# Layer 1's value product in a two-layer transformer kernel: the first key tile in three rounded products

## The chip, the core and the metric

The kernel runs on one NeuronCore of one Trainium2 chip. The metric is the device time of one execution in microseconds; the median of 3 runs of the kernel before is 726.27 us (725.91 to 726.91). The engines work side by side and meet by semaphores: TensorE (PE) multiplies and transposes, VectorE (DVE) and ScalarE (ACT) work element by element, GpSimd (POOL) prepares weights, SyncE (SP) starts the loads. Results of TensorE arrive in PSUM, which has eight banks here used for one purpose each.

## The reference, cut to what matters

Four sequences of 256 tokens with 256 features pass through two pre-norm layers of attention and feed-forward. The change is in layer 1's attention: 16 heads of 128, causal.

```python
k = jnp.einsum('ihd,bpd->biph', W_K, x)
q = jnp.einsum('ihd,bpd->biph', W_Q, x)
v = jnp.einsum('ihd,bpd->biph', W_V, x)
scores = jnp.einsum('biph,biqh->biqp', k, q)
mask = jnp.tril(jnp.ones((pos, pos), dtype=x.dtype))
masked = scores * mask - jnp.float32(10000000000.0) * (1.0 - mask)
attn = jax.nn.softmax(masked / jnp.sqrt(jnp.float32(d_head)), axis=-1)
z = jnp.einsum('biqp,biph->biqh', attn, v)
z_flat = jnp.transpose(z, (0, 2, 1, 3)).reshape(b, pos, -1)
out = jnp.einsum('df,bqf->bqd', W_O, z_flat)
```

## The kernel before

The attention of a layer is 64 units: 8 head pairs, and in each pair 4 sequences times 2 heads. A unit is one sequence and one head, 256 queries against 256 keys. Since the mask is causal, the first tile of 128 keys meets all 256 queries and the second only the last 128, so probabilities are 384 columns a unit. All engines run the same sequence of slots, numbered -5 to 70. Slots -5 to 10 are written out, slots 11 to 58 are three rounds of a loop of 16 slots, and the rest is written out again. In slot c each engine works on several units at different ages: TensorE does the scores of unit c, the query/key projection and the value projection of step c + 5, the output projection of unit c - 6 (from slot 6 on), the transposes of the probabilities of unit c - 2, and the value product of unit c - 3, in that order. What orders the engines among each other are counting semaphores: `need` waits until a step of a unit is done. Each engine goes through its own list strictly in order, so a wait holds up all that stands behind it.

Weights and normalised tokens are held as two fp32r tensors each, a main part (hi, the value rounded to fp32r) and a remainder (lo, the difference, also rounded). A product of two such values is three products: hi by hi, hi by lo, lo by hi (`PASSES`). Scores and value products are plain fp32. A value projection writes bank 4 (`TQ_BANK`), and ScalarE copies it to `v` (L454); TensorE may write the next one once that copy is done (`vev`). The turned probabilities go to bank 5 (`PT_BANK`) and ScalarE copies them to `probs_t` (L412). The value product (L330 for the first key tile, L332 for the second) adds into bank 6, from where ScalarE takes the main part of the encoded values (L425) and VectorE the remainder (L500). VectorE's slot is: normalise the probabilities of unit c - 1 (L480, L483), add the output to the residual (L491), `enc_lo` (L500), maxima of the scores of unit c (L519).

At slots -4 to -2 of layer 1 the end of layer 0's feed-forward still runs on VectorE and TensorE: the sparse selection (work, L921 to L929) and the last down-projection (L723). L382 is layer 1's query/key projection, L396 its value projection, L304 the output projection, L316 the transposes, L282 and L283 the scores.

Of the kernel before, what the change touches and what calls it, by code (L numbers as in the profile page):

```python
# [29 lines left out]
P = 128  # L30
D = 256
# [20 lines left out]
SECOND_OUTPUT_FROM, SECOND_OUTPUT_TQ = UNITS - 10, UNITS - 6  # L52
HI_HI, HI_LO, LO_HI = (0, 0), (0, 1), (1, 0)
# [17 lines left out]
def need_pairs(eng, sem, it, c, per_pair):  # L71

    if it is not None:
        eng.wait_ge(sem, it * (2 * per_pair) + c)
    elif c > 0:
        eng.wait_ge(sem, c)

def build(nc, x_in, wa, wax, wb, wdown0, w2t, consts, scales, out):
    with ExitStack() as ctx:  # L80
# [3 lines left out]
        def sem(name):  # L84
# [28 lines left out]
        rot_a = sb("rot_a", [P, 2, 384])  # L113
        rot_b = sb("rot_b", [P, 2, 384])
        cos_t = sb("cos_t", [P, 2, 3, DH])
        sin_t = sb("sin_t", [P, 2, 3, DH])

# [29 lines left out]
        w2_a = sb("w2_a", [P, 8, D])  # L147
        w2_b = work[:, 0:8 * D].rearrange("p (a d) -> p a d", d=D)
# [10 lines left out]
                 "a0hi", "a0", "ahi", "a", "bhi", "b")  # L159
# [126 lines left out]
        def pe_output(pe, L, it, c):  # L286
# [3 lines left out]
            if live(it, m):  # L290
# [6 lines left out]
                elif m == SECOND_OUTPUT_TQ:  # L297
                    pe.wait_ge(s["tqev" if L == 0 else "vev"], UNITS)
                elif m > SECOND_OUTPUT_FROM:
                    pe.wait_ge(s["opadd"], m - 1)  # L300
                else:
                    need(pe, s["opadd"], it, m)
# [5 lines left out]
        def pe_turn_probs(pe, L, it, c):  # L308
# [3 lines left out]
            if live(it, m):  # L312
                need(pe, s["pnorm"], it, 2 * m + 2, 2)
                need(pe, s["ptev"], it, m)
                for j in range(3):
# [3 lines left out]
        def pe_values(pe, L, it, c):  # L319
# [3 lines left out]
            if live(it, m):  # L323
# [6 lines left out]
                pe.matmul(bank[O_BANK][:, 0:256], v[:, m // 8 % 2, 2 * b, vc:vc + DH], probs_t[:, m % 2, 0:256],  # L330
                          start=True, stop=False, skip_group_check=True)
# [16 lines left out]
        def pe_slot(pe, L, it, c):  # L348
# [38 lines left out]
            if L == 1:  # L387

                m = c + 5
                if live(it, m):  # L390
# [3 lines left out]
                    need(pe, s["vev"], it, m)  # L394
                    for i, (g, (l, r)) in enumerate([(g, p) for g in range(NC) for p in PASSES]):
# [10 lines left out]
        def act_turned(act, L, it, m):  # L406

            s = at[L]
            if live(it, m):
                need(act, s["pt"], it, m + 1)  # L410
                need(act, s["pv"], it, m - 1)
                nc.scalar.copy(probs_t[:, m % 2, :], bank[PT_BANK][:, 0:384]).then_inc(s["ptev"], 1)  # L412

        def act_slot(act, L, it, c):
# [12 lines left out]
            if live(it, m):  # L427
# [8 lines left out]
                else:  # L436
# [14 lines left out]
                    elif it is None and m == 8:  # L451

                        act.wait_ge(ff[0]["down"], 12)
                    nc.scalar.copy(v[:, m // 8 % 2, t, :], bank[TQ_BANK][:, 0:D]).then_inc(s["vev"], 1)  # L454
# [47 lines left out]

        def dve_scores_wait(dve, L, it, c):
# [19 lines left out]
        def dve_slot(dve, L, it, c):  # L523
            s = at[L]
            if c < TAIL_SLOT:
                dve_normalise(dve, L, it, c)
                dve_residual(dve, L, it, c)
                dve_scores_wait(dve, L, it, c)
# [12 lines left out]
            if live(it, m):  # L541
                t = m % 8
                if L == 0:
# [932 lines left out]
```

## Time and profile before

| | |
|---|---|
| median of 3 runs | 726.27 us |
| the profiled execution, its own time | 726.39 us |
| its span | 724.6 us |
| TensorE busy | 702.7 us, 97% |
| VectorE busy | 495.1 us, 68% |
| ScalarE busy | 407.7 us, 56% |
| GpSimd busy | 353.3 us, 49% |
| chain that ended last | TensorE 93% |

Busy times of TensorE come from records that overlap, since a product begins before the one ahead has drained; spacing of starts, or the chain of waits, tells what a product costs. "PEld" is the loading of weights, which runs beside the products. An fp32 product is recorded as two instructions of each kind. A line number names the line of the kernel that issued the instruction. "idle before" is how long the engine stood ahead of an instruction, and the releaser is what it waited for.

### The profile page before, as it was taken

The numbers are of one execution on the slowest core, as the hardware profiler recorded it, in microseconds if no ns is written. First come the engines' busy times: TensorE is split into PE (matmuls) and PEld (weight loads), VectorE is DVE, ScalarE is ACT, GpSimd is POOL, SyncE is SP. The second block draws the span as 40 slices with busy tenths as digits, with TensorE's granted clock in tenths as the row PEclk, the third lists the DMA queues.
The fourth block names the chain that finished last, engine by engine and source line by source line (L and its number), as shares of the span: only waits on it lengthen the run. The fifth ranks groups of instructions, "written<-read, shape, count | busy, mean of one in ns | idle before, by whom it ended". The sixth has DMA issues, their size and how long they took to land.

```text
span 724.6 us, 14870 instructions
## 1 busy us (share of the span) xinstructions
PE 702.7 (97%) x4296; PEld 627.5 (87%) x4296; DVE 495.1 (68%) x1698; ACT 407.7 (56%) x1214; POOL 353.3 (49%) x503
## 2 busy tenths in 40 slices
PE   4799999999999998999999999999999999999998
PEld 3589999999999997788889999999999999987887
DVE  6998888888888889869755554444444444587443
ACT  4576666667676674523246555555555555664221
POOL 3898888878888853202069842323232323018000
PEclk9999999999999999999999999999999999999999
DMA  6010210101020010100021010101010200000000
GB/s 232 2 44 2 103 45 1 43 0 43 0 101 29 29 67 7 45 1 0 16 88 59 1 59 1 59 7 52 14 44 26 75 0 0 0 1 1 1 30 29
DMA packets 9002, 24.64 MB, mean 34 GB/s; under 512 B 896, under 2 KB 3072, under 8 KB 8832
## 3 DMA queue, kind: packets, MB, share of 16 engines
q1 hardware_dynamic: 8240, 22.55, 8.9%
q10 hardware_dynamic: 720, 1.57, 0.6%
q8 instruction: 21, 0.34, 0.2%
q14 instruction: 21, 0.17, 0.1%
HBM read 23.07 MB, written 1.05 MB: 33 GB/s over the span
## 4 chain that ended last, share of the span: by engine, by line
PE 93%; DVE 3%; POOL 1%; issue 1%; DMA 1%; ACT 0%; ACTq 0%; DVEq 0%; POOLq 0%
PE bank L382 12%; PE bank L664 12%; PE bank L304 12%; PE bank L376 11%; PE bank L330 7%; PE bank L283 7%; PE bank L396 6%; PE bank L316 6%; PE bank L282 4%; PE bank L332 4%; PE bank L703 3%; PE bank L345 3%; PE bank L707 2%; PE bank L723 1%; PE bank L243 1%
## 5 line engine op out<-in xcount | busy, mean ns | idle before, releaser
L471 ACT ACTIVATE probs<-scores,negmax 128x128 f32<-128x128 f32 (+1 forms) x256 | 115.5, 452 | 40.8 <-DVE negmax L519 40.1
L500 DVE TENSOR_TENSOR enc_lo<-bank,enc_hi 128x256 fp32r<-128x256 f32 x128 | 54.2, 424 | 116.7 <-PE bank L283 113.2
L412 ACT COPY probs_t<-bank 128x384 f32<-128x384 f32 x128 | 61.3, 479 | 122.8 <-PE bank L316 122.8
L565 POOL TENSOR_TENSOR a_hi<-raw_a,zero 128x384 fp32r<-128x384 f32 (+1 forms) x60 | 43.7, 728 | 86.8 <-PE bank L396 86.8
L483 DVE TENSOR_SCALAR probs<-probs,rinv 128x128 f32<-128x128 f32 (+1 forms) x256 | 80.8, 357 | 4.5
L330 PE MATMUL bank<-probs_t,v 128*128 128x256 f32 x256 | 76.6, 381 | 0.1
L283 PE MATMUL bank<-qk 128*128 128x256 f32 x256 | 76.5, 380 | 0.0
L229 POOL TENSOR_TENSOR ln_r<-ln_ve,neg_half 128x1 f32<-128x1 f32 x24 | 15.5, 644 | 123.8 <-DVE ln_ve L207 123.8
L578 POOL TENSOR_TENSOR rms_r<-meansq,neg_half 128x3 f32<-128x3 f32 x64 | 58.3, 911 | 34.5 <-DVE meansq L555 34.3
L304 PE MATMUL bank<-b_hi,enc_hi 128*128 128x256 f32 x256 | 74.3, 290 | 0.2 <-DVE x L491 0.2
L304 PE MATMUL bank<-b_hi,enc_lo 128*128 128x256 f32 x256 | 72.3, 282 | 0.0
L304 PE MATMUL bank<-b_lo,enc_hi 128*128 128x256 f32 x256 | 72.3, 282 | 0.0
L376 PE MATMUL bank<-a_hi,xT_hi 128*128 128x512 f32 x128 | 62.3, 486 | 4.9 <-DVE xT_lo L256 4.0
L580 POOL TENSOR_TENSOR rot_a<-rot_a,rot_b 128x384 f32<-128x384 f32 x64 | 66.4, 1038 | 0.0
L316 PE MATMUL bank<-cst,probs 128*128 128x128 f32 x384 | 63.0, 272 | 0.0
L425 ACT CAST enc_hi<-bank 128x256 fp32r<-128x256 f32 x128 | 47.6, 372 | 25.5 <-PE bank L332 25.4
L382 PE MATMUL bank<-xT_hi,a_hi 128*128 128x512 f32 x128 | 61.5, 481 | 0.3 <-DVE xT_lo L256 0.3
L567 POOL TENSOR_TENSOR a_lo<-raw_a,a_hi 128x384 fp32r<-128x384 f32 (+1 forms) x60 | 54.8, 914 | 4.7
L332 PEld LDWEIGHTS bank<-probs_t,v 128*128 128x128 f32 x256 | 48.6, 190 | 6.6
L491 DVE TENSOR_TENSOR x<-bank,x 128x256 f32<-128x256 f32 x128 | 53.1, 415 | 0.0
L304 PEld LDWEIGHTS bank<-b_hi,enc_hi 128*128 128x128 f32 x256 | 48.4, 189 | 4.4 <-issue 0.3
L304 PEld LDWEIGHTS bank<-b_lo,enc_hi 128*128 128x128 f32 x256 | 48.3, 189 | 4.4
(130 smaller groups left out, 2056.5 us busy)
## 6 DMA issues: line engine op xcount, KB each, us to landing
raw_a<-in_wa SPq DMA_DIRECT2D x10, 768.0 KB, 4.4
raw_a<-in_wa SPq DMA_DIRECT2D x9, 512.0 KB, 4.2
raw_b<-in_wb SPq DMA_DIRECT2D x16, 256.0 KB, 2.6
x<-in_x SPq DMA_DIRECT2D x4, 256.0 KB, 5.8
hid_last<-in_wax SPq DMA_DIRECT2D x2, 512.0 KB, 4.8
w_a<-in_w2t SPq DMA_DIRECT2D x1, 1024.0 KB, 4.8
raw_b<-in_wdown SPq DMA_DIRECT2D x2, 512.0 KB, 3.3
raw_a<-in_wa ACTq DMA_DIRECT2D x1, 512.0 KB, 5.1
```

What stands on the lines that cost most here:

```text
L283: pe.matmul(ps[:, 128:384], qk[:, q, t0 + 128:t0 + 256], qk[:, k, t0:t0 + 256], start=True, stop=True).then_inc(s["scores"], 1)
L304: mm = pe.matmul(output_bank(m)[:, 0:D], enc[l][:, h, t * P:(t + 1) * P], b_w[slot][r][:, h * D:(h + 1) * D], start=i == 0, stop=i == 5)
L316: mm = pe.transpose(bank[PT_BANK][:, j * P:(j + 1) * P], probs[:, m % 4, j * P:(j + 1) * P], ident)
L330: pe.matmul(bank[O_BANK][:, 0:256], v[:, m // 8 % 2, 2 * b, vc:vc + DH], probs_t[:, m % 2, 0:256], start=True, stop=False, skip_group_chec ...
L332: pe.matmul(bank[O_BANK][:, 128:256], v[:, m // 8 % 2, 2 * b + 1, vc:vc + DH], probs_t[:, m % 2, 256:384], start=False, stop=True, skip_gr ...
L376: mm = pe.matmul(ps[:, :], xT[l][:, g, t * P:(t + 1) * P], a_w[slot][r][:, g * 512:(g + 1) * 512], start=i == 0, stop=i == 5)
L382: mm = pe.matmul(ps[:, :], a_w[slot][l][:, g * 768 + w * P:g * 768 + (w + 1) * P], xT[r][:, g, half * 512:(half + 1) * 512], start=i == 0, ...
L412: nc.scalar.copy(probs_t[:, m % 2, :], bank[PT_BANK][:, 0:384]).then_inc(s["ptev"], 1)
L471: nc.scalar.activation(probs[:, c % 4, c0:c1], scores[:, c % 2, c0:c1], ACT.Exp, bias=negmax[:, c % 2, r:r + 1], scale=-1.0, accum_out=row ...
L483: nc.vector.tensor_scalar(probs[:, m % 4, c0:c1], probs[:, m % 4, c0:c1], rinv[:, m % 4, r:r + 1], None, ALU.mult).then_inc(s["pnorm"], 1)
L580: nc.gpsimd.tensor_tensor(rot_a[:, m % 2, :], rot_a[:, m % 2, :], rot_b[:, m % 2, :], ALU.add).then_inc(s["radd"], 1)
L664: mm = pe.matmul(ps[:, :], a_w[t][l][:, c0:c0 + P], xT[rr][:, g, th * 512:(th + 1) * 512], start=q == 0, stop=q == 5)
```

## The change

For the first seven head pairs of layer 1 (units 0 to 55) the value product of the first key tile, one fp32 product, becomes three fp32r products of main parts and remainders; the last eight units and the second key tile stay fp32. For this
- ScalarE copies the first 256 columns of the turned probabilities to `turned` (main part) and the other 128 to `probs_t`, two instructions for one; VectorE subtracts to get the remainder (`dve_turned_lo`), between the residual and `enc_lo`, and signals `ptlo`;
- of each second value tile (the first key tile of a sequence, t even) ScalarE writes a main part ahead of its copy to `v`, and VectorE makes the remainder at the end of its slot, behind the maxima, and signals `vlo`. This is done for all 32 such tiles, the last pair's too;
- TensorE waits for `ptlo` ahead of the transposes (they write the bank that the subtraction reads) and ahead of the value product, and for `vlo` ahead of the value product and of the value projection (which writes the bank that the subtraction reads).

The parts of the values lie in `v_early`, which with `turned` takes the place of layer 0's rotation tensors, and in the upper half of `b_w`, which the attention left unused. The diff, without its empty lines and with little of what surrounds it:

```diff
@@ -50,6 +50,7 @@
 SECOND_OUTPUT_FROM, SECOND_OUTPUT_TQ = UNITS - 10, UNITS - 6
+SPLIT_VALUES = UNITS - 8
 HI_HI, HI_LO, LO_HI = (0, 0), (0, 1), (1, 0)
@@ -74,6 +75,11 @@
+def in_parts(L, it, m):
...
+    return L == 1 and (it is not None or m < SPLIT_VALUES)
@@ -110,11 +116,6 @@
         rms_r = sb("rms_r", [P, TILES, 3])
-        rot_a = sb("rot_a", [P, 2, 384])
-        rot_b = sb("rot_b", [P, 2, 384])
-        cos_t = sb("cos_t", [P, 2, 3, DH])
-        sin_t = sb("sin_t", [P, 2, 3, DH])
@@ -145,6 +146,26 @@
+        with ExitStack() as first_layer:
+            def sb0(name, shape):
+                return first_layer.enter_context(nc.sbuf_tensor(name, shape, F32))
...
+            rot_a = sb0("rot_a", [P, 2, 384])
+            rot_b = sb0("rot_b", [P, 2, 384])
+            cos_t = sb0("cos_t", [P, 2, 3, DH])
+            sin_t = sb0("sin_t", [P, 2, 3, DH])
+        v_early = sb("v_early", [P, 2, 2, 512], F32R)
+        turned = sb("turned", [P, 2, 2, 256], F32R)
...
+        def v_part(part, slot, e):
...
+            if e < 2:
+                return v_early[:, slot, part, e * D:(e + 1) * D]
+            return b_w[slot][part][:, WB + (e - 2) * D:WB + (e - 1) * D]
         w2_b = work[:, 0:8 * D].rearrange("p (a d) -> p a d", d=D)
@@ -156,7 +177,7 @@
                  "proj", "vproj", "qkev", "vev", "sq", "ss", "ms", "rp", "rot", "radd", "roped", "tq", "tqev",
-                 "a0hi", "a0", "ahi", "a", "bhi", "b")
+                 "a0hi", "a0", "ahi", "a", "bhi", "b", "ptlo", "vlo")
         at = [{n: sem(f"L{L}_{n}") for n in names} for L in range(2)]
@@ -296,6 +317,8 @@
                     pe.wait_ge(s["tqev" if L == 0 else "vev"], UNITS)
+                    if L == 1:
+                        pe.wait_ge(s["vlo"], UNITS // 2)
                 elif m > SECOND_OUTPUT_FROM:
@@ -312,6 +335,8 @@
                 need(pe, s["ptev"], it, m)
+                if L == 1:
+                    need(pe, s["ptlo"], it, m if it is not None else min(m, SPLIT_VALUES))
                 for j in range(3):
@@ -327,8 +352,15 @@
                 need(pe, s["elo"], it, m)
-                pe.matmul(bank[O_BANK][:, 0:256], v[:, m // 8 % 2, 2 * b, vc:vc + DH], probs_t[:, m % 2, 0:256],
-                          start=True, stop=False, skip_group_check=True)
+                if in_parts(L, it, m):
+                    need(pe, s["ptlo"], it, m + 1)
+                    need_pairs(pe, s["vlo"], it, (m - hh + 2) // 2, 4)
+                    for i, (l, r) in enumerate(PASSES):
+                        pe.matmul(bank[O_BANK][:, 0:256], v_part(l, m // 8 % 2, b)[:, vc:vc + DH], turned[:, r, m % 2, :],
+                                  start=i == 0, stop=False, skip_group_check=True)
+                else:
+                    pe.matmul(bank[O_BANK][:, 0:256], v[:, m // 8 % 2, 2 * b, vc:vc + DH], probs_t[:, m % 2, 0:256],
+                              start=True, stop=False, skip_group_check=True)
                 pe.matmul(bank[O_BANK][:, 128:256], v[:, m // 8 % 2, 2 * b + 1, vc:vc + DH], probs_t[:, m % 2, 256:384],
@@ -392,6 +424,7 @@
                     need(pe, s["vev"], it, m)
+                    need_pairs(pe, s["vlo"], it, (m + 1) // 2, 4)
                     for i, (g, (l, r)) in enumerate([(g, p) for g in range(NC) for p in PASSES]):
@@ -409,7 +442,11 @@
                 need(act, s["pv"], it, m - 1)
-                nc.scalar.copy(probs_t[:, m % 2, :], bank[PT_BANK][:, 0:384]).then_inc(s["ptev"], 1)
+                if in_parts(L, it, m):
+                    nc.scalar.copy(turned[:, 0, m % 2, :], bank[PT_BANK][:, 0:256])
+                    nc.scalar.copy(probs_t[:, m % 2, 256:384], bank[PT_BANK][:, 256:384]).then_inc(s["ptev"], 1)
+                else:
+                    nc.scalar.copy(probs_t[:, m % 2, :], bank[PT_BANK][:, 0:384]).then_inc(s["ptev"], 1)
@@ -451,6 +488,8 @@
                         act.wait_ge(ff[0]["down"], 12)
+                    if t % 2 == 0:
+                        nc.scalar.copy(v_part(0, m // 8 % 2, t // 2), bank[TQ_BANK][:, 0:D])
                     nc.scalar.copy(v[:, m // 8 % 2, t, :], bank[TQ_BANK][:, 0:D]).then_inc(s["vev"], 1)
@@ -500,6 +539,14 @@
+        def dve_turned_lo(dve, L, it, m):
...
+            s = at[L]
+            if live(it, m) and in_parts(L, it, m):
+                need(dve, s["ptev"], it, m + 1)
+                nc.vector.tensor_tensor(turned[:, 1, m % 2, :], bank[PT_BANK][:, 0:256], turned[:, 0, m % 2, :].bitcast(F32),
+                                        ALU.subtract).then_inc(s["ptlo"], 1)
@@ -525,6 +572,7 @@
                 dve_residual(dve, L, it, c)
+                dve_turned_lo(dve, L, it, c - 3)
                 dve_scores_wait(dve, L, it, c)
@@ -540,6 +588,10 @@
                 t = m % 8
+                if L == 1 and t % 2 == 0:
+                    need(dve, s["vev"], it, m + 1)
+                    nc.vector.tensor_tensor(v_part(1, m // 8 % 2, t // 2), bank[TQ_BANK][:, 0:D],
+                                            v_part(0, m // 8 % 2, t // 2).bitcast(F32), ALU.subtract).then_inc(s["vlo"], 1)
                 if L == 0:
```

TensorE in slot 10, the last ahead of the loop, from the value projection to the value product (bank4 is `TQ_BANK`, bank5 `PT_BANK`; the number behind a weight's name is its buffer), before:

```order
L396 MATMUL bank4<-a_hi1,xT_hi 128x256 [waits L1_vev]
L396 MATMUL bank4<-a_lo1,xT_hi 128x256
L396 MATMUL bank4<-a_hi1,xT_lo 128x256
L396 MATMUL bank4<-a_hi1,xT_hi 128x256
L396 MATMUL bank4<-a_lo1,xT_hi 128x256
L396 MATMUL bank4<-a_hi1,xT_lo 128x256
L316 MATMUL bank5<-cst,probs 128x128 [waits L1_ptev,L1_pnorm]
L316 MATMUL bank5<-cst,probs 128x128 x2
L330 MATMUL bank6<-probs_t,v 128x256 [waits L1_elo,L1_vev,L1_ptev]
L332 MATMUL bank6<-probs_t,v 128x128
```

and with the change:

```order
L429 MATMUL bank4<-a_hi1,xT_hi 128x256 [waits L1_vlo,L1_vev]
L429 MATMUL bank4<-a_lo1,xT_hi 128x256
L429 MATMUL bank4<-a_hi1,xT_lo 128x256
L429 MATMUL bank4<-a_hi1,xT_hi 128x256
L429 MATMUL bank4<-a_lo1,xT_hi 128x256
L429 MATMUL bank4<-a_hi1,xT_lo 128x256
L341 MATMUL bank5<-cst,probs 128x128 [waits L1_ptlo,L1_ptev,L1_pnorm]
L341 MATMUL bank5<-cst,probs 128x128 x2
L359 MATMUL bank6<-turned,b_hi0 128x256 [waits L1_ptlo,L1_elo,L1_vlo,L1_vev,L1_ptev]
L359 MATMUL bank6<-turned,b_hi0 128x256
L359 MATMUL bank6<-turned,b_lo0 128x256
L364 MATMUL bank6<-probs_t,v 128x128
```

The value projection waits for the values' remainder besides the copy, the transposes for the probabilities' remainder, and the fp32 product into bank6 is now three products with five waits.

VectorE in slot 10 (an even one), from the residual to the end of the slot, before:

```order
L491 TENSOR_TENSOR x<-bank7,x 128x256 [waits L1_op]
L500 TENSOR_TENSOR enc_lo<-bank6,enc_hi 128x256 [waits L1_ehi,L1_exp,L1_scores]
L519 ISA scores,negmax<-bank0,cst 128x128
L519 ISA negmax 128x1
L519 ISA scores,negmax<-bank0,cst 128x256
L519 ISA negmax 128x1
```

and with the change:

```order
L530 TENSOR_TENSOR x<-bank7,x 128x256 [waits L1_op]
L547 TENSOR_TENSOR turned<-bank5,turned 128x256 [waits L1_ptev]
L539 TENSOR_TENSOR enc_lo<-bank6,enc_hi 128x256 [waits L1_ehi,L1_exp,L1_scores]
L566 ISA scores,negmax<-bank0,cst 128x128
L566 ISA negmax 128x1
L566 ISA scores,negmax<-bank0,cst 128x256
L566 ISA negmax 128x1
L593 TENSOR_TENSOR b_lo1<-bank4,b_hi1 128x256 [waits L1_vev]
```

One subtraction stands ahead of enc_lo in each slot. In even slots a second one, with the wait for ScalarE's copy of the values, stands behind the maxima.

VectorE at slots -4 and -3 of layer 1, in the sparse selection of layer 0, before:

```order
L916 TENSOR_SCALAR work<-work 128x512 [waits F0_cmp]
L917 TENSOR_TENSOR work<-work 128x512
L918 TENSOR_TENSOR work<-work 128x512
L921 TENSOR_TENSOR work<-work 128x512 [waits beaten_sums]
L922 TENSOR_TENSOR work<-work 128x512
L929 SCALAR_TENSOR_TENSOR hid_last<-work,hid_last 128x1024 [waits votes] x2
L892 TENSOR_TENSOR x<-bank6,x 128x256 [waits F0_down]
```

and with the change:

```order
L968 TENSOR_SCALAR work<-work 128x512 [waits F0_cmp]
L969 TENSOR_TENSOR work<-work 128x512
L970 TENSOR_TENSOR work<-work 128x512
L593 TENSOR_TENSOR v_early<-bank4,v_early 128x256 [waits L1_vev]
L973 TENSOR_TENSOR work<-work 128x512 [waits beaten_sums]
L974 TENSOR_TENSOR work<-work 128x512
L981 SCALAR_TENSOR_TENSOR hid_last<-work,hid_last 128x1024 [waits votes] x2
L593 TENSOR_TENSOR v_early<-bank4,v_early 128x256 [waits L1_vev]
L944 TENSOR_TENSOR x<-bank6,x 128x256 [waits F0_down]
```

The first subtraction of values, with its wait for ScalarE, stands ahead of the votes and of the product with the mask (hid_last), the second one behind them and ahead of layer 0's last residual additions.

## Rows read from the trace of the kernel before

**Rows 1.** The page: busy time of the engines; the granted clock in 40 slices.

```profile
PE 702.7 (97%) x4296; PEld 627.5 (87%) x4296; DVE 495.1 (68%) x1698; ACT 407.7 (56%) x1214; POOL 353.3 (49%) x503
...
PEclk9999999999999999999999999999999999999999
```

**Rows 2.** Table of stretches: busy us of each engine, clock, DMA share.

```profile
394.00:620.00 226.00, 226.00 (x1472) 207.88 (x1471) 107.65 (x454) 131.27 (x404) 81.76 (x112) 1.00 0.08 27
```

**Rows 3.** Waits from 395 to 636 us: us in total, times, longest.

```profile
DVE enc_lo L500 <- PE bank L283: 84.2, 53, 1.9
ACT probs_t L412 <- PE bank L316: 79.4, 55, 1.6
```

**Rows 4.** Chain of waits from 395 to 405 us: start, us, what.

```profile
395.10 0.33 PE bank L316 x3
395.42 0.43 PE bank L330 x2
395.86 0.22 PE bank L332 x2
...
396.74 1.39 PE bank L382 x6
398.12 0.71 PE bank L304 x6
398.83 0.71 PE bank L396 x6
```

**Rows 5.** Timeline of an even slot: start, us, instruction [idle before <-releaser].

```profile
480.30 0.48 ACT L412 COPY probs_t<-bank 128x384 f32<-128x384 f32 x1 [1.50 <-PE bank L316]
...
480.96 0.37 ACT L425 CAST enc_hi<-bank 128x256 fp32r<-128x256 f32 x1 [0.18 <-PE bank L332]
...
481.23 0.59 ACT L441 COPY qk<-bank 128x512 f32<-128x512 f32 x1
...
481.70 0.39 ACT L454 COPY v<-bank 128x256 f32<-128x256 f32 x1
...
482.51 0.08 DVE L519 DVE_READ_ACCUMULATOR2_ANT negmax<- 128x1 f32 x1
...
483.52 0.28 PE L396 MATMUL bank<-a_hi,xT_hi 128*128 128x256 f32 x1
...
483.97 0.41 DVE L491 TENSOR_TENSOR x<-bank,x 128x256 f32<-128x256 f32 x1
...
486.26 0.42 DVE L500 TENSOR_TENSOR enc_lo<-bank,enc_hi 128x256 fp32r<-128x256 f32 x1 [1.88 <-PE bank L283]
```

**Rows 6.** Timeline ahead of the loop, slots -4, -3, 0, 1, 2 and 4.

```profile
354.30 0.37 ACT L454 COPY v<-bank 128x256 f32<-128x256 f32 x1
...
354.81 2.35 DVE L929 SCALAR_TENSOR_TENSOR hid_last<-work,hid_last 128x1024 f32<-128x1024 uint8 x2
...
355.51 0.28 PE L396 MATMUL bank<-a_hi,xT_hi 128*128 128x256 f32 x1
...
358.34 1.02 PE L723 MATMUL bank<-raw_b,hid_last 128*128 128x256 f32 x4
...
372.81 0.37 ACT L454 COPY v<-bank 128x256 f32<-128x256 f32 x1
...
373.99 0.28 PE L396 MATMUL bank<-a_hi,xT_hi 128*128 128x256 f32 x1
...
376.37 0.36 PE L396 MATMUL bank<-a_hi,xT_hi 128*128 128x256 f32 x1
...
379.13 0.08 DVE L519 DVE_READ_ACCUMULATOR2_ANT negmax<- 128x1 f32 x1
379.20 0.28 PE L396 MATMUL bank<-a_hi,xT_hi 128*128 128x256 f32 x1
...
385.74 0.08 DVE L519 DVE_READ_ACCUMULATOR2_ANT negmax<- 128x1 f32 x1
...
386.02 0.28 PE L396 MATMUL bank<-a_hi,xT_hi 128*128 128x256 f32 x1
```

## The prediction

> **What bounds the kernel now.** I read the page first: TensorE is busy 97% of the span at a granted clock of full speed [rows 1]. The table of stretches then says that from 394 to 620 us, the repeating part of layer 1, TensorE is busy for all 226.00 of 226.00 us [rows 2]. The list of waits over the same part shows who has time: VectorE stood 84.2 us before the remainder of the encoded values and ScalarE 79.4 us before the copy of the turned probabilities, both waiting for TensorE, and TensorE waited for nobody [rows 3]. So in this stretch the time is the sum of TensorE's spacings, which the chain of waits gives without the overlap of the pipelined records [rows 4]. One slot (one head of one batch) is 0.33 (transposes) + 0.43 + 0.22 (value product, 256 and 128 columns) + 0.22 + 0.43 (scores) + 1.39 + 0.71 + 0.71 = about 4.45 us. The scores' two rows repeat those of the value product and are not shown.
>
> **What is taken from TensorE.** The fp32 product with 256 columns costs 0.43 us (recorded as two instructions) [rows 4]. It becomes three fp32r products of 256 columns. The same kind stands in the output projection, six in 0.71 us, and in the value projection, six in 0.71 us [rows 4]: 0.119 us each, 0.356 us for three. Saving 0.43 - 0.356 = 0.075 us for a unit. The split runs for m below 56: 8 units in the slots ahead of the loop, 48 in the loop's three rounds. 56 x 0.075 = 4.2 us. Bounds: TensorE already changes between fp32 and fp32r twice in each slot, and the six projections behind the fp32 scores still take 1.39 us [rows 4], so the two new changes of kind should cost nothing; if all rounding of the rows fell one way (0.44 against 0.354, or 0.425 against 0.360) the saving would be 4.8 or 3.6 us. I take 4.2.
>
> The row: 0.43 us for one fp32 product and 0.119 us for one fp32r product of the same width, a ratio of 3.6. The Trainium skill, FP8 and Floating Point Precision, section TensorE Precision Notes, says that true fp32 takes 4 passes, all four cross products. By that rule three products are three quarters of it, 0.11 us less per unit, an estimate of 6.0 us; the row's ratio gives less, and the sum goes by the row.
>
> **What is added beside TensorE, in the loop.** I follow the even slot of rows 5, whose scores began at 480.76.
> ScalarE: the copy of 384 columns (0.48) becomes one of 256 (0.37 to 0.39, as the casts and copies of rows 5) and one of 128. The cast at 480.96 and the copy behind it at 481.23 start 0.27 apart, so the pair ends about 0.1 us later than 480.78, beside the cast's own wait for TensorE. Of the value copies, each second one is doubled: the copy at 481.70 is preceded by a cast, so the value copy ends at 482.38 to 482.5 instead of 482.09. ScalarE then has some 0.6 us more in an even slot of 4.4 and had 79.4 us of wait in 55 slots [rows 3], 1.4 each.
> VectorE: the remainder of the turned probabilities, one subtraction of 0.42 us (as the enc_lo row) [rows 5], waits for the copies until about 485.5 in the next slot. Behind it are enc_lo and the maxima, which waited until 486.26 in any case (VectorE's last residual ended at 484.38 [rows 5], and 84.2 us over 53 waits is 1.6 each [rows 3]). TensorE wants this remainder only in the next round of transposes, over 2 us later. So it costs nothing; without that cover it would be 0.42 us a unit.
> The remainder of the values is the tight one. It stands at the end of VectorE's even slot, behind the maxima, and the value projection of the next tile, which writes the same PSUM bank, now waits for it. Behind that projection on TensorE stand the transposes and everything else. Maxima end at 482.59, + 0.42 + a signal of under 0.1 = 483.1; the projection's first product is at 483.52 [rows 5], its weight load some 0.12 ahead of it (the spacing of such pairs). Slack 0.3 us: nothing in the loop. The output projection, 0.71 us long and between scores and value projection, gives this slack.
>
> **Ahead of the loop there is no such cover**, since the output projection begins only with slot 6. Four places [rows 6], each in TensorE's own time:
> - Slot -4: the value copy ran at 354.30; behind a cast it ends at about 354.97, the subtraction at 355.4, the projection that stood at 355.51 starts at 355.7. Cost 0.2 (with the first product behind a pause 0.36 long instead of 0.28). On VectorE the last steps of the sparse selection of layer 0 stand behind this new wait: their first product with the mask, 354.81, moves 1.2 us and the second half ends at 358.4. TensorE's last down-projection starts at 358.34 and wants that half only at its third product, 0.87 later, so 0 us; the cover left is 0.7 us.
> - Slots 0 and 1: the copy at 372.81 gets a cast ahead of it. The projection at 373.99 comes 0.1 to 0.2 later, and the exponentials with their table load 0.29 later, so that the one at 376.37, which waited for ScalarE before, comes 0.3 later in all. Cost 0.3.
> - Slot 2: maxima ended at 379.21, the projection stood at 379.20. With the subtraction it is 379.13 + 0.42 + 0.06 + 0.12 for the weight load: 0.5 to 0.6 later.
> - Slot 4: maxima end at 385.82, projection at 386.02: now 386.4. Cost 0.4.
> Slots 3 and 5 have no new subtraction. The sum is 0.2 + 0.3 + 0.55 + 0.4 = 1.45 us. Bounds: 0, if the following stretches take it back (they are full [rows 2], so hardly), and 2.5 us if the shifts of ScalarE and VectorE add where I let them overlap. I take 1.4. SBUF tiles that change place, four value casts of the last pair that nobody reads, and the unsplit last eight units cost TensorE nothing. No DMA, and no instruction of POOL or SP, is added or moved past another.
>
> **Sum.** 726.39 (the profiled execution) - 4.2 + 1.4 = 723.6 us; it stands 0.12 above the median of the runs, so 723.5 for the median.
>
> **Rivals.**
> A, the head start costs nothing: TensorE's delays are hidden. 726.3 - 4.2 = 722.1 us. For it: 0.28 us of pause existed ahead of 376.37. Against: rows 6 show maxima and projection back to back in slots 2 and 4.
> B, the values' remainder is late in the loop as well. 24 even slots of the loop; each 0.1 us past the slack of 0.3 costs 2.4 us. At 0.4 us late instead of 0.3 early, a sum near 726 us: no change. For it: VectorE's chain through maxima is paced by TensorE's scores, and nothing can move it forward. Against: it needs 0.4 us of extra time that no row has.
> C, slower: TensorE cannot take the new waits without a pause. In each slot the transposes get one more wait, the value product two, each second value projection one, and in the loop they are compared with registers. The row of a restart is the one at 376.37: 0.36 us for a product that otherwise takes 0.28 [rows 6]. Two such pauses in each of 56 slots are 56 x 0.16 = 9.0 us, giving 726.3 - 2.8 + 9.0 = 732.5 us. It becomes slower than before from 0.05 us a slot on. Against: transposes with two waits and the value product with three follow each other at 0.33 and 0.43 without a gap [rows 4], in the loop as ahead of it.
>
> **How the numbers follow.** Forecast 0.62 (722.7 to 724.8), A 0.15, B 0.12, C 0.11. About 0.2% (1.45 us) is what a measurement can tell from no change. Faster 0.78: the forecast, A and a little of B. Same 0.12, slower 0.10. Range 721.8 to 726.8: down to A with the larger saving, up into B; C and the rest are left out.
>
> **What would show it.** In the profile after: the three new products in a chain of 0.36 us behind transposes of 0.33, a slot of 4.38 instead of 4.46 us, and TensorE still without idle time from 394 us on. In the head, idle time ahead of the value projection put down to VectorE's new subtraction, about 1.4 us in four places. VectorE's enc_lo wait falls by about 0.4 a slot. Wrong would be: a wait of TensorE ahead of the value projection in the loop's even slots (B), a spacing above 0.12 between the new products or gaps ahead of transposes (C), or no idle time in slots 2 and 4 (A).

## The result: 722.6 us, 0.55% faster, and the profile after

The changed kernel takes 722.62 us (median of 5 runs, 722.34 to 723.48) against 726.27. The ratio is 0.9945, 95% interval 0.9935 to 0.9956. The prediction was 723.5 us with a range of 721.8 to 726.8, so the sign is right, the time lies in the range, and it is 0.9 us below the number.

The page has the instructions that the change adds: TensorE 56 (4296 before), VectorE 88, ScalarE 88, GpSimd none [rows 1]. The second line is of the table of stretches, 394 to 620 us, which answers to [rows 2].

```profile
PE 698.4 (97%) x4352; PEld 625.5 (87%) x4352; DVE 529.5 (73%) x1786; ACT 417.6 (58%) x1302; POOL 353.3 (49%) x503
```

```profile
394.00:620.00 226.00, 226.00 (x1551) 210.11 (x1550) 140.39 (x540) 141.37 (x488) 82.39 (x112) 1.00 0.08 27
```

TensorE is still busy for every microsecond of the repeating part. VectorE has 32.7 us more work in it and ScalarE 10.1 us more, and neither shows in TensorE. The chain of waits answers to [rows 4] (start, us, what). In the new numbering L341 is the transposes, L359 the three new products, L364 the narrow fp32 product, L303 and L304 the scores, L414 the projection, L327 the output projection, L429 the value projection.

```profile
395.54 0.33 PE bank L341 x3
395.87 0.36 PE bank L359 x3
396.23 0.22 PE bank L364 x2
396.45 0.22 PE bank L303 x2
396.67 0.43 PE bank L304 x2
397.11 1.39 PE bank L414 x6
398.50 0.72 PE bank L327 x6
399.21 0.72 PE bank L429 x6
```

Only the second line changed, 0.43 to 0.36. The list of waits over 395 to 636 us answers to [rows 3].

```profile
ACT turned L446 <- PE bank L341: 76.9, 52, 1.6
...
DVE turned L547 <- ACT probs_t L447: 42.9, 48, 1.0
...
DVE enc_lo L539 <- PE bank L304: 14.0, 52, 1.6
```

VectorE's wait moved: 1.59 us a slot before enc_lo became 0.27 there and 0.89 before the new subtraction (L547), 0.43 us less together. TensorE has no line in the list but one of 0.2 us.

To find where the time went, I took the start of the second projection matmul of every slot from the timelines and set each kernel against the kernel before, both counted from slot -5. Positive is later than before, in us; I call this number the drift. The experiments e1 to e12 are told in the next section; e1 is the same program as "after", and its row is the same within 0.03.

```
slot        -3     0     1     2     3     4     5     8     9    26    58
after     +.10  +.06  +.22  +.29  +.63  +.55  +.83  +.62  +.55  -.82 -3.38
e3        -.04  -.05  -.02  -.05  -.06  -.06  +.31  +.32 +1.09         -2.60
e4        -.03  -.04  -.02  -.38  -.38  -.46  -.53  -.74  -.82 -2.09 -4.65
e5        +.10  +.10  +.25  +.31  +.63  +.64 +1.01  +.99 +2.13        +2.11
e8        +.09  +.08  +.24  +.31  +.63  +.56  +.85  +.61  +.54  +.68 +1.60
e9        +.11  +.10  +.25  +.32  +.65  +.69 +1.09 +1.20 +2.20        +3.58
e10       +.11  +.07  +.22  +.29  +.61  +.62  +.98  +.96  +.98         +.98
e11       -.03  -.05  -.03  -.06  -.07  -.07  +.30  +.29  +.30        -3.45
e12       +.11  +.08  +.24  +.31  +.63  +.55  +.84  +.62  +.55        -3.38
```

Read along its row, "after" loses in five steps before the loop (slots -4, 0, 1, 2 and 4; each shows in the column of the next slot), about 1.0 us, and gains 0.08 a slot where the split product runs. At slot 58 it is 3.38 ahead: 4.4 gained, 1.0 lost. The rest of its profiled execution, 3.9 us shorter in span, is 0.33 us that it was ahead before layer 1's first slot and 0.2 us after slot 58. But for 0.08 of the last split unit, both lie in code that the change doesn't touch.

Two of the four places of [rows 6], slots -4 and 2, look like this in the timeline (start, us, instruction, idle before; L492 is the added cast, L493 the value copy, L593 the new subtraction of the values).

```profile
353.98 0.37 ACT L492 CAST v_early<-bank 128x256 fp32r<-128x256 f32 x1
354.25 0.38 ACT L493 COPY v<-bank 128x256 f32<-128x256 f32 x1
...
354.66 0.43 DVE L593 TENSOR_TENSOR v_early<-bank,v_early 128x256 fp32r<-128x256 f32 x1 [0.89 <-ACT v L493]
...
355.23 0.35 PE L429 MATMUL bank<-a_hi,xT_hi 128*128 128x256 f32 x1
...
378.89 0.41 DVE L593 TENSOR_TENSOR b_lo<-bank,b_hi 128x256 fp32r<-128x256 f32 x1
...
379.42 0.19 PEld L429 LDWEIGHTS bank<-a_hi,xT_hi 128*128 128x128 f32 x1 [0.51 <-issue]
379.45 0.36 PE L429 MATMUL bank<-a_hi,xT_hi 128*128 128x256 f32 x1
```

In slot 2 the weight load of the value projection starts 0.53 us after the subtraction started and 0.12 after it ended, and the first product 0.03 after the load. The chain of waits shows slot 4 in the same way: 0.95 us for six products that take 0.71 elsewhere.

```profile
386.44 0.10 issue
386.55 0.95 PE bank L429 x6
```

The prediction expected the profile to name the subtraction as what these loads waited for. It does not. Over 352 to 394 us it puts the idle time of the value projection's weight load down to "issue" (time in which the engine waited for nothing that the profile shows), once before and five times after. First the kernel before, then the changed one (us in total, times, longest):

```profile
PEld bank L396 <- issue: 0.5, 1, 0.5
```

```profile
PEld bank L429 <- issue: 2.2, 5, 0.6
```

That the new wait is what TensorE stands for is shown by e3 and e4 below.

In the loop there is slack. The timeline of an even slot has the subtraction over at 481.80 and the projection at 482.38.

```profile
481.38 0.42 DVE L593 TENSOR_TENSOR b_lo<-bank,b_hi 128x256 fp32r<-128x256 f32 x1
...
482.38 0.28 PE L429 MATMUL bank<-a_hi,xT_hi 128*128 128x256 f32 x1
```

### The profile page after: what moved, and what is told of

Its sections match the earlier page's. It is cut to its first block, busy times and chain, and to the rows that moved or that the text cites. A ratio compares the mean times of both kernels' runs of the same rounds, so it can differ in the third digit from the quotient of the medians.

```text
span 720.7 us, 15291 instructions
## 1 busy us (share of the span) xinstructions
PE 698.4 (97%) x4352; PEld 625.5 (87%) x4352; DVE 529.5 (73%) x1786; ACT 417.6 (58%) x1302; POOL 353.3 (49%) x503
## 4 chain that ended last, share of the span: by engine, by line
PE 92%; DVE 4%; issue 1%; POOL 1%; DMA 1%; ACT 0%; ACTq 0%; DVEq 0%; POOLq 0%
PE bank L414 12%; PE bank L327 12%; PE bank L716 11%; PE bank L408 11%; PE bank L304 7%; PE bank L429 7%; PE bank L341 6%; PE bank L362 4%; PE bank L303 4%; PE bank L364 4%; PE bank L755 3%; PE bank L359 3%; PE bank L377 3%; PE bank L759 2%; PE bank L775 1%
## 5 line engine op out<-in xcount | busy, mean ns | idle before, releaser
L304 PE MATMUL bank<-qk 128*128 128x256 f32 x256 | 76.5, 381 | 0.0
L327 PE MATMUL bank<-b_hi,enc_hi 128*128 128x256 f32 x256 | 73.9, 289 | 0.1
L327 PE MATMUL bank<-b_lo,enc_hi 128*128 128x256 f32 x256 | 72.3, 282 | 0.0
L327 PE MATMUL bank<-b_hi,enc_lo 128*128 128x256 f32 x256 | 72.3, 282 | 0.0
L446 ACT CAST turned<-bank 128x256 fp32r<-128x256 f32 x56 | 20.8, 372 | 80.6 <-PE bank L341 80.6
L341 PE MATMUL bank<-cst,probs 128*128 128x128 f32 x384 | 63.0, 273 | 0.0
L414 PE MATMUL bank<-xT_hi,a_hi 128*128 128x512 f32 x128 | 61.6, 482 | 0.3 <-DVE xT_lo L277 0.3
L449 ACT COPY probs_t<-bank 128x384 f32<-128x384 f32 x72 | 34.4, 478 | 42.5 <-PE bank L341 42.4
L547 DVE TENSOR_TENSOR turned<-bank,turned 128x256 fp32r<-128x256 f32 x56 | 23.8, 424 | 44.2 <-ACT probs_t L447 44.0
L833 ACT ACTIVATE gate<-bank 128x512 f32<-128x512 f32 x32 | 19.1, 598 | 58.2 <-PE bank L716 58.1
L327 PEld LDWEIGHTS bank<-b_hi,enc_hi 128*128 128x128 f32 x256 | 48.5, 189 | 4.5 <-issue 0.3
```

What stands on the lines that cost most here:

```text
L304: pe.matmul(ps[:, 128:384], qk[:, q, t0 + 128:t0 + 256], qk[:, k, t0:t0 + 256], start=True, stop=True).then_inc(s["scores"], 1)
L327: mm = pe.matmul(output_bank(m)[:, 0:D], enc[l][:, h, t * P:(t + 1) * P], b_w[slot][r][:, h * D:(h + 1) * D], start=i == 0, stop=i == 5)
L341: mm = pe.transpose(bank[PT_BANK][:, j * P:(j + 1) * P], probs[:, m % 4, j * P:(j + 1) * P], ident)
L414: mm = pe.matmul(ps[:, :], a_w[slot][l][:, g * 768 + w * P:g * 768 + (w + 1) * P], xT[r][:, g, half * 512:(half + 1) * 512], start=i == 0, ...
```

## The experiments

Twelve kernels ran in three groups, each group on one chip with its own runs of the kernel before (726.47, 726.83 and 726.91 us). Line numbers differ by a few between them.

**e1 and e2: how much is chance, how much is layout.** e1 is the changed kernel again. e2 is the kernel before with the changed kernel's SBUF tiles, none of the new instructions:

```
-        rot_a = sb("rot_a", [P, 2, 384])          (and rot_b, cos_t, sin_t)
+        with ExitStack() as first_layer:  ...     (the four, as in the change)
+        v_early = sb("v_early", [P, 2, 2, 512], F32R)
+        turned = sb("turned", [P, 2, 2, 256], F32R)
```

> The changed kernel once more, beside the others of this group. My reading of the two traces: 56 units at 0.0785 us gained (4.4 us), about 1.0 us lost in four places ahead of the loop, and about 0.3 us that the trace after is already ahead when layer 1 begins. Expected 722.6 us.

> The kernel before with the changed kernel's placement of tensors in SBUF and nothing else. The changed kernel's trace is 0.33 us ahead before layer 1 begins, where no instruction differs. If that is the spread of single executions, this runs at 726.3 us, no different from before. Rival: the placement of tensors gives those 0.3 us, and this runs at 725.9 to 726.0 us.

e1: 722.61 us (721.55 to 722.82), ratio 0.9946, interval 0.9933 to 0.996. e2: 725.89 us (725.35 to 726.84), ratio 0.9993, 0.9984 to 1.0002. The gain repeats. The layout gives nothing that can be told from no change, but the measured 725.89 is the rival's number, and the interval allows a gain of up to 1.2 us: that the layout gives 0.3 us is neither shown nor excluded. The profiled executions of the changed kernel and of e1, one and the same program, reach slot -5 at 351.92 and 350.91 us: equal code spreads by about a microsecond ahead of layer 1, more than the 0.33 us in question.

**e5: the waits and copies alone.** The three products become one fp32 product of the main parts (so their remainders are left out of the result); every cast, subtraction and wait stays.

```
-  for i, (l, r) in enumerate(PASSES):
-      pe.matmul(..., v_part(l, ...)[:, vc:vc + DH], turned[:, r, m % 2, :], start=i == 0, ...)
+  pe.matmul(..., v_part(0, ...)[...].bitcast(F32), turned[:, 0, m % 2, :].bitcast(F32), start=True, ...)
```

> The changed kernel with all its copies, subtractions and waits, but with one fp32 product of the two main parts in place of the three fp32r products (the remainders' products are left out of the result). This is the cost of the change without its gain. By my theory 726.27 + 1.0 (ahead of the loop) = 727.3 us, or 727.0 if the placement of tensors gives 0.3. My prediction's price was 1.4: 727.7. Rival: waits or copies cost something in every slot of the loop as well, 0.05 us a slot and more: 730 us or above.

728.9 us (727.75 to 729.04), ratio 1.0025, 1.0015 to 1.0036: 2.1 us slower than before, where 0.7 to 1.0 was expected. The table says which part missed. Up to slot 8 the drift is +0.99, the cost ahead of the loop. From slot 9 to 58 it stands at +2.11 to +2.13, so the loop costs nothing. Between them is one jump of 1.14 us that my theory did not have.

**e3: the first head pair not split.** It gives up 8 units and with them the additions of slots -4, 0 and 2.

```
-    return L == 1 and (it is not None or m < SPLIT_VALUES)
+    return L == 1 and (it is not None or 8 <= m < SPLIT_VALUES)
```

(The counts of the waits, the value casts and the value subtractions are changed to match.)

> The changed kernel, with the first head pair (units 0 to 7) left as one fp32 product and its value parts not made. By my theory the new waits at slots -4, 0 and 2 go (0.12 + 0.2 + 0.34 = 0.66 us) and 8 x 0.0785 = 0.63 us of the gain go with them: 722.6 us, the same as the changed kernel. Rival: those delays come from something else than the wait for the values' remainder and stay; then 723.2 us. By my prediction's larger prices (1.05 us for these slots) it would be 722.2.

724.27 us, ratio 0.9972, 0.996 to 0.9983: a miss by 1.7 us. The steps of slots -4 to 2 are gone and the one of slot 4 stayed, 0.37, as expected. But between slots 8 and 9 there is again a jump, 0.77 us. The timeline there (VectorE and GpSimd):

```profile
397.64 1.01 POOL L619 TENSOR_TENSOR a_lo<-raw_a,a_hi 128x384 fp32r<-128x384 f32 x1
...
397.73 3.41 DVE L522 TENSOR_SCALAR probs<-probs,rinv 128x128 f32<-128x128 f32 x2
...
398.61 2.38 POOL L1171 TENSOR_TENSOR work<-w_a 128x1024 f32<-128x1024 f32 x1
...
402.27 0.41 DVE L593 TENSOR_TENSOR b_lo<-bank,b_hi 128x256 fp32r<-128x256 f32 x1
...
402.84 0.36 PE L429 MATMUL bank<-a_hi,xT_hi 128*128 128x256 f32 x1 [0.27 <-DVE b_lo L593]
```

Two normalise operations that usually take 0.55 us together take 3.41. The view of that line alone gives them apart (ns min, median, max):

```profile
L522 DVE TENSOR_SCALAR probs<-probs,rinv x2: 1004/1743/2482, 397.7 to 398.7; 128x128 f32<-128x128 f32 x1, 128x256 f32<-128x256 f32 x1
```

The first lasts until GpSimd's a_lo is done, the second until GpSimd's 2.4-us operation is done. Everything behind on VectorE is late, at last the subtraction that the value projection waits for. Both projections of the slot were held up: the weight load of the output projection was idle 0.42 us, that of the value projection 0.45. e5 shows 3.44 us at 399.64 with the same operation beside it. In the kernel before and in the changed one the normalise starts ahead of a_lo and gets through. The kernel before:

```profile
398.72 0.55 DVE L483 TENSOR_SCALAR probs<-probs,rinv 128x128 f32<-128x128 f32 x2
...
399.00 1.13 POOL L567 TENSOR_TENSOR a_lo<-raw_a,a_hi 128x384 fp32r<-128x384 f32 x1
...
400.10 2.40 POOL L1119 TENSOR_TENSOR work<-w_a 128x1024 f32<-128x1024 f32 x1
```

The changed kernel, where the normalise also starts while GpSimd's a_hi is still running:

```profile
398.45 0.84 POOL L617 TENSOR_TENSOR a_hi<-raw_a,zero 128x384 fp32r<-128x384 f32 x1
...
399.09 0.56 DVE L522 TENSOR_SCALAR probs<-probs,rinv 128x128 f32<-128x128 f32 x2
```

The Trainium skill, SBUF — State Buffer, section SBUF: two separate sides, says that VectorE, in a mode that uses two ports or with two inputs in SBUF, and GpSimd share one pair of ports under an exclusive lock, held for a whole instruction by whichever starts first. No row here shows in which mode the normalise runs. The rows of e3 agree with the lock: each normalise ends 0.08 and 0.15 us behind the end of one GpSimd instruction. The last two rows do not fit it as they stand: there the normalise takes its usual time though a_hi, which had started first, ran 0.20 us into it by the records (those of GpSimd are rough). Its a_lo starts at 399.38, 0.29 behind the normalise.

**e10, e11, e12: three kernels (e5, e3, the changed one) without GpSimd's long operations.** This tests the cause of the jumps.

```
-  nc.gpsimd.tensor_tensor(b[:, :, n % 2, :], a[:, :, 0, :], a[:, :, 1, :], ...)
+  nc.gpsimd.tensor_tensor(b[:, :, n % 2, 0:32], a[:, :, 0, 0:32], a[:, :, 1, 0:32], ...)
```

> The kernel of the one fp32 product, with GpSimd's six 2.4-us operations of 128x1024 (layer 1's slots 5 to 10, the Hadamard steps for w2) cut to a few columns, so w2 of FFN 1 isn't made. Theory: the 1.14 us that this kernel lost in slots 8 and 9 came of VectorE's normalise operations being held 3.4 us while such an operation ran on GpSimd. Then the jump goes: drift at slot 9 stays near +1.0 instead of +2.13, no normalise takes over 1 us, and the time is 727.8 us. Rival: the jump comes of where the copies and waits stand, GpSimd has no part: it stays, 728.9 us.

> The kernel whose first head pair is left whole, with the same GpSimd operations cut. Theory: its jump of 0.77 us in slots 8 and 9 goes, the drift at slot 58 falls from -2.60 to about -3.4, and the time is 723.5 us. Rival: 724.3 us, nothing moves.

> The changed kernel with the same GpSimd operations cut, as the measure for the two runs before it. Theory: in the changed kernel the normalise slips in between GpSimd's operations, so little is held, and cutting them gives 0 to 0.4 us (722.3 to 722.6; a normalise of slots 8 and 9 stays at 0.56). If the cut itself gave as much as 0.8 to 1.1 us here too, the gain in the two runs before it would not be that of their jumps.

e10: 727.6 us (ratio 1.0011, 1.0001 to 1.0021); e11: 723.02 (0.9951, 0.9935 to 0.9968); e12: 723.01 (0.9949, 0.9932 to 0.9965). In the table the jumps of e10 and e11 at slot 9 are gone (+0.96 to +0.98, +0.29 to +0.30) and e12's line is that of the changed kernel to 0.02. The rival, that GpSimd has no part, falls. GpSimd's other operations move forward with the cut, a_lo too, so these runs do not tell what each of the two operations beside the normalise cost. The normalise of e10 at the place of the jump, in the timeline:

```profile
398.55 0.55 DVE L521 TENSOR_SCALAR probs<-probs,rinv 128x128 f32<-128x128 f32 x2
```

e12 itself is 0.4 us above what I expected, within its runs' spread. e11 equals e12, so apart from the collision splitting the first head pair is worth nothing: 8 units gain 0.64 and the slots ahead of it cost 0.68. One thing stays open: the jump of e3 in its profiled execution is 0.8 us, while the ratios of e3 and e11 differ by 1.5 us. Their intervals allow both numbers, but the profiled execution of e3 took 723.02 us and is the fastest of its seven; the other six took 723.98 to 724.78. So the jump accounts for about half of the 1.7 us by which e3 missed. What the slower executions did is not shown.

**e6: are waits free?** (rival C)

```
   need(pe, s["ptlo"], it, m if it is not None else min(m, SPLIT_VALUES))     (transposes)
+  need(pe, s["exp"], it, 2 * m + 2, 2)
+  need(pe, s["rinv"], it, m + 1)
   need_pairs(pe, s["vlo"], it, (m - hh + 2) // 2, 4)                         (value product)
+  need(pe, s["exp"], ...); need(pe, s["rinv"], ...); need(pe, s["pnorm"], ...); need(pe, s["pt"], ...)
```

> The changed kernel with six more semaphore waits of TensorE in each slot that are always fulfilled by then: four ahead of the value product, two ahead of the transposes. If the waits themselves cost TensorE nothing, 722.6 us as the changed kernel. Rival C (a wait lets TensorE run dry): the change added three to four a slot, so at 0.05 us for each such place this runs at 728 us or above.

722.85 us (722.53 to 723.09), ratio 0.9946, 0.993 to 0.9961. Its drift at slot 58 is -3.38, that of the changed kernel, and the chain has the same numbers (L343 transposes, L365 new products):

```profile
395.71 0.33 PE bank L343 x3
396.03 0.35 PE bank L365 x3
```

Six more fulfilled waits in each slot cost nothing, so the few that the change added cannot have. Rival C is refuted.

**e7 and e8: how much slack has the values' remainder in the loop?** (rival B) One or two subtractions of the same size stand ahead of it in the loop's even slots.

```
+  for k in range(1 if it is not None else 0):      (2 in e8)
+      nc.vector.tensor_tensor(gate[:, k, ...], bank[TQ_BANK][:, 0:D], v_part(0, ...).bitcast(F32), ALU.subtract)
   nc.vector.tensor_tensor(v_part(1, m // 8 % 2, t // 2), ...).then_inc(s["vlo"], 1)
```

> The changed kernel with one more subtraction of the same size (to a scratch tile) ahead of the values' remainder on VectorE in the loop's 24 even slots. The trace after shows the remainder 0.46 us ahead of the weight load that waits for it. One more takes 0.34 to 0.42 us: still in time, 722.6 us, at most 0.5 more. Rival B (the loop has no slack there): 24 x 0.4 = 9.6 us more, 732 us.

> The same with two more subtractions: 0.68 to 0.84 us against 0.46 of slack, 0.22 to 0.38 us late in each of 24 even slots. By my theory 5.3 to 9.1 us more: 728 to 732 us. If it stays at 722.6, the value projection isn't what the remainder holds up.

e7: 722.78 us, ratio 0.9948, 0.9932 to 0.9963: no change. e8: 727.79 us (727.27 to 728.55), ratio 1.0015, 1.0006 to 1.0024: the whole gain is gone. In its timeline the two additions push the remainder 0.67 us behind the last record of the maxima (482.68), and TensorE names it:

```profile
483.35 0.41 DVE L596 TENSOR_TENSOR b_lo<-bank,b_hi 128x256 fp32r<-128x256 f32 x1
483.81 0.19 PEld L429 LDWEIGHTS bank<-a_hi,xT_hi 128*128 128x128 f32 x1 [0.17 <-DVE b_lo L596]
```

The chain of waits has 0.95 us instead of 0.71 for the value projection of this slot:

```profile
483.14 0.70 PE bank L327 x6
483.84 0.95 PE bank L429 x6
```

Its drift at slot 58 is +1.60 against -3.38, 5.0 us from the 23 even slots of the loop ahead of it, 0.22 each. The remainder came 0.67 us later and cost 0.22, so the slack was 0.45 us. Rival B's mechanism is real, and its place was right; it only begins 0.45 us further on.

**e4: another bank ahead of the loop.** The value projections of steps 1, 5, 7 and 9 write bank 7, idle until the output projection begins, so they need not wait for the copies and the subtraction of the bank ahead. (The waits are changed to match.)

```
+SIDE_STEPS = (1, 5, 7, 9)
+        def value_bank(it, m):
+            return bank[OP_BANK if it is None and m in SIDE_STEPS else TQ_BANK]
-                        mm = pe.matmul(bank[TQ_BANK][:, 0:D], xT[l] ...
+                        mm = pe.matmul(value_bank(it, m)[:, 0:D], xT[l] ...
```

> The changed kernel, with value projections 1, 5, 7 and 9 written to the output projection's PSUM bank, which is idle ahead of slot 6, so that they wait neither for the copy nor for the remainder of the tile ahead. By my theory the four delays (1.0 us) go, and the 0.28 us pause that was there before in slot 1 as well: 721.3 to 721.6 us. Rival: ScalarE and VectorE are late by themselves there, TensorE waits at the next step instead, and it stays at 722.6 us.

721.28 us (720.87 to 721.7), ratio 0.9928, 0.9914 to 0.9942: 1.3 us less than the changed kernel on the same chip. Its chain through slot 4 has no pause:

```profile
384.02 1.39 PE bank L423 x6
385.41 0.71 PE bank L444 x6
386.12 0.33 PE bank L350 x3
```

Its drift is -4.65 at slot 58, 1.27 better than the changed kernel's. At slot 9 it was 1.37 better: 0.36 of that is a pause of slot 1 that the kernel before has too, and the other 1.0 is what the change cost there. This shows that the cost ahead of the loop is the wait for the shared bank. It is the fastest version here.

**e9: what does a narrow rounded product cost?** The narrow fp32 product becomes three rounded ones of 128 columns. They use the first key tile's parts, so the last tile's contribution is not computed.

```
-  pe.matmul(bank[O_BANK][:, 128:256], v[...], probs_t[:, m % 2, 256:384], start=False, stop=True, ...)
+  for l, r in PASSES:
+      pe.matmul(bank[O_BANK][:, 128:256], v_part(l, ...), turned[:, r, m % 2, 128:256], ...)
```

> The other value product of each of the first seven head pairs, the one fp32 product of 128 columns for the last key tile (0.22 us in the changed kernel's chain), is made as three rounded products of 128 columns as well, of parts that are there already. What a rounded product costs at 256 columns is 0.119 us (0.36 for three). If that is a price by columns, three of 128 take 0.18 us and a unit gains 0.04: 56 units give -2.2 us, 720.4 us. If it is a floor for each product with its weight load, three take 0.36 us, a unit loses 0.14: 56 x 0.14 = +7.8, 730.4 us. In the chain the group of three shows 0.18 or 0.36.

729.68 us (729.16 to 730.53), ratio 1.0044, 1.0027 to 1.0061. The floor is right in kind: a unit loses 0.108 us (the drift grows by 0.028 a slot where the changed kernel's falls by 0.080), 0.22 + 0.108 = 0.33 us for three, 0.109 each, if all of the loss is put down to them. 56 x 0.108 = 6.0, and the jump at slot 9 came too (3.31 us for the normalise at 399.12), 1.0: 7.0 of the 7.1 us measured. The chain spreads the loss over two lines, 0.06 each (both 0.22 in the changed kernel): the three products themselves take 0.28, 0.093 each, and the rest stands in the score product behind them. Why that one is longer is not shown.

```profile
482.15 0.36 PE bank L359 x3
482.50 0.28 PE bank L366 x3
482.79 0.28 PE bank L303 x2
```

## Why the prediction came out right, step by step

**TensorE is the bound and everything else hides in the loop: right.** e5 shows it alone: from slot 9 to 58 its drift stands still at +2.12 with every new copy, subtraction and wait in place.

**The gain of a unit: 0.075 predicted, 0.080 measured**, 4.5 us against 4.2 for 56. The difference lies within the rounding of the rows. By the Trainium skill's four-pass rule (FP8 and Floating Point Precision, section TensorE Precision Notes) it would have been 0.11, an estimate; the measurement goes with the row. The price of a rounded product is not in step with its columns: 0.109 us at most for 128 (e9), 0.119 for 256, and 0.23 for 512 (six in 1.39). Between 128 and 256 columns it hardly changes, and from there it nearly doubles. Why three of 256 come to 0.356 and not to three quarters of 0.43 is not shown.

**The stretch ahead of the loop costs 1.4: the term that was mis-sized; 1.0 measured.** The places were right (e3 removes the first three of them, e4 nearly all). Slot -4 took 0.12 where I had 0.2, slots 0 and 1 took 0.22 (0.3), slot 2 0.34 (0.55), slot 4 0.36 (0.4). The step that failed is the sum of slots 0 to 2. I took each price in TensorE's own time and added them, as if the maxima of slot 2 came later by what slots 0 and 1 had cost. They don't: in the timeline VectorE goes from the normalise straight into them, in the changed kernel

```profile
377.78 0.64 DVE L522 TENSOR_SCALAR probs<-probs,rinv 128x128 f32<-128x128 f32 x2
378.34 0.28 DVE L566 CUSTOM_DVE_ANT_0 scores<-bank,cst 128x128 f32<-128x128 f32 x1
```

and in the kernel before

```profile
378.00 0.66 DVE L483 TENSOR_SCALAR probs<-probs,rinv 128x128 f32<-128x128 f32 x2
378.58 0.28 DVE L519 CUSTOM_DVE_ANT_0 scores<-bank,cst 128x128 f32<-128x128 f32 x1
```

so VectorE's own chain sets their time, and TensorE's delay so far only ate into its lead. Before the change the last record of the maxima started 1.08 us behind TensorE's second projection matmul of slot 2 (379.13 and 378.05), after it 0.86 us behind (378.89 and 378.03). That is 0.22 less, which is what slots 0 and 1 had cost. 0.55 - 0.22 = 0.33, against 0.34 measured: the two waits overlap.

**Slack of 0.3 us for the values' remainder: right in sign, 0.45 in size** (e7 and e8). The subtraction starts together with the last record of the maxima (both 481.38), where I let it start 0.08 behind, and in e8 TensorE's load follows its end by 0.05 (483.76 to 483.81), where I allowed 0.1; in slot 2 of the changed kernel it was 0.12.

**Rivals.** A (the cost ahead of the loop hidden, 722.1) lies nearer to the measured 722.6 than my 723.5, yet its mechanism is refuted: the pauses stand in the chain, and e4 gets them back. The median lies 0.9 us under my number because 0.3 more was gained and 0.4 less was lost; the last 0.2 lies outside the changed stretches, and whether chance or the layout gave it stays open. B was not near: with one more subtraction in place (0.33 us) 0.12 us of slack was left, and e8 shows its price once it starts. My condition for it was misstated: at 2.4 us for each 0.1 us past the slack, a sum near 726 needs the remainder 0.1 us late, that is 0.4 later than I had it, and not 0.4 late, which would cost 9.6 us. C fell with e6. The estimate of 0.124 us for a load and a product beside it falls with e9, whose pairs of 128 columns take 0.109 us at most.

**What I did not see**: the time depends on where VectorE's normalise falls against GpSimd's long operations in slots 5 to 10. It cost the changed kernel nothing, by luck of phase, but three of the other kernels (e3, e5, e9) paid 0.8 to 1.1 us. Being held is not yet a cost. The changed kernel's normalise took 1.89 us at 407.86 and its drift shows no step there. In e4 it took 2.37:

```profile
406.48 2.37 DVE L537 TENSOR_SCALAR probs<-probs,rinv 128x128 f32<-128x128 f32 x2
```

and that slot lasted 4.50 us instead of 4.38, a cost of 0.1. So in these two slots a hold of 1.9 us was covered in full and one of 2.4 not quite. The trace of before had the hold to be seen:

```profile
407.63 1.74 DVE L483 TENSOR_SCALAR probs<-probs,rinv 128x128 f32<-128x128 f32 x2
```

## What to carry to other kernels

Where one engine is busy all the time, price a change by the spacings of that engine in the chain of waits, and then look for stretches where an operation that usually lies between two others is missing: there the new wait has no cover, and the head start of a pipeline is such a stretch. A result bank that gains one more reader can delay its next writer, as it did here ahead of the loop, so look for an idle bank to alternate with. When an experiment misses by a constant, follow the drift slot by slot against the kernel before: a step is something that happened once (here a wait ahead of the loop, or the collision with GpSimd), a slope is a price.

## What the runs showed of the hardware that I had not expected

- VectorE's normalise (SBUF to SBUF) was held by GpSimd's a_lo and by its 128x1024 operations: 0.55 us for two became 3.31 to 3.44, and in e3 each ended just behind a GpSimd instruction. In these five runs it went by which started first: 0.28 and 0.29 us ahead of a_lo (before, after) the normalise got through, 0.06 to 0.19 us behind (e5, e3, e9) it was held, and that cost 0.8 to 1.1 us of the kernel's time. No run lies between. Beside a_hi it took its usual 0.56 us in the changed kernel.
- A rounded product of 128 columns costs 0.093 to 0.109 us beside 0.119 for 256 columns. So three of them in place of one fp32 product gained at 256 columns (0.43 to 0.36) and lost at 128 (0.22 to 0.33).
- Six more fulfilled waits in TensorE's queue in each slot, in the loop compared with registers, cost nothing (e6).
